# Ternary weights turned by transposing DMA instead of by TensorE, in a fused graph-and-expert layer

## What is computed

```python
def _bit_quant(W):
    scale = jnp.clip(jnp.mean(jnp.abs(W), axis=-1, keepdims=True), 1e-05, None)
    w_q = jnp.clip(jnp.round(W / scale), -1.0, 1.0) * scale
...
shared_out = jax.nn.silu(jnp.einsum('btd,fd->btf', h, sw1)) @ sw2.T
...
h1 = jax.nn.silu(jnp.einsum('btd,efd->ebtf', h, ew1))
eo = jnp.einsum('ebtf,edf->ebtd', h1, ew2)
```

## Time and profile before

| | |
|---|---|
| median of 3 runs | 772.42 us |
| the profiled execution | 770.02 us, span 768.4 us |
| TensorE busy | 691.9 us, 90% of the span |
| VectorE busy | 502.9 us, 65% |
| ScalarE busy | 409.0 us, 53% |
| GpSimd busy | 199.9 us, 26% |
| moved by DMA | 145.69 MB, mean 190 GB/s |

### The profile page before, as it was taken

One profiled execution on the slowest core, in us unless ns is written; L12 is line 12 of the kernel. 1 busy time (PEld: TensorE's weight loads), 2 busy tenths in 40 slices (PEclk: granted clock), 3 DMA queues, 4 the chain that ended last, 5 costly groups with the idle time before them and its releaser, 6 DMA issues.

```text
span 768.4 us, 17793 instructions
## 1 busy us (share of the span) xinstructions
PE 691.9 (90%) x5737; PEld 412.7 (54%) x5738; DVE 502.9 (65%) x1111; ACT 409.0 (53%) x716; POOL 199.9 (26%) x195
## 2 busy tenths in 40 slices
PE   0889988999999999999887669899989999999996
PEld 0334433554544554544333357677766777777773
DVE  4888876546655546788888776765674545454554
ACT  2334346759977775867466635335344444444441
POOL 1222210000000000177656433520020543434332
PEclk9999999999999999999989979999999999999999
DMA  8999951433546878767555554255338544444431
GB/s 354 420 376 378 351 199 40 151 140 110 192 171 234 279 261 283 231 218 224 201 197 192 192 179 154 82 184 163 120 112 110 154 138 129 132 132 124 133 108 36
DMA packets 55585, 145.69 MB, mean 190 GB/s; under 512 B 8814, under 2 KB 8814, under 8 KB 51440
## 3 DMA queue, kind: packets, MB, share of 16 engines
q1 hardware_dynamic: 41792, 115.64, 44.3%
q0 software_dynamic: 6960, 20.99, 8.5%
q10 hardware_dynamic: 6784, 8.42, 3.5%
HBM read 127.69 MB, written 19.16 MB: 191 GB/s over the span
## 4 chain that ended last, share of the span: by engine, by line
PE 58%; issue 14%; DVE 11%; DMA 6%; ACT 5%; POOL 4%; ACTq 1%; DVEq 1%; SPq 0%; POOLq 0%
PE bank L1417 17%; PE bank L1441 15%; PE bank L1280 7%; PE bank L1282 7%; PE bank L1281 7%; DMA work<-in_w 4%; PE bank L1314 2%; POOL dv L519 2%; PE bank L1404 2%; ACT junk L670 2%; DVE work L991 2%; DVE region L1086 1%; DVE work L1058 1%; DVE s L979 1%; ACT region L678 1%
## 5 line engine op out<-in xcount | busy, mean ns | idle before, releaser
L1441 PE MATMUL bank<-region,work 128*128 (+1 forms) x624 | 142.9, 383 | 5.1 <-DVE work L1140 3.6
L1417 PE MATMUL bank<-work,region 128*128 128x128 f16 x1984 | 118.4, 221 | 4.1 <-ACT work L794 2.9
L1417 PEld LDWEIGHTS bank<-work,region 128*128 (+1 forms) x1984 | 114.7, 99 | 10.5 <-issue 3.4
L1280 PE MATMUL bank<-zreg,work 128*128 (+1 forms) x256 | 98.8, 386 | 13.5 <-DVE work L1058 11.2
L1280 PE MATMUL bank<-region,work 128*128 128x512 f16 (+1 forms) x192 | 74.8, 390 | 29.4 <-DVE region L914 29.3
L1140 DVE SCALAR_TENSOR_TENSOR work<-work 128x512 f16<-128x512 f32 x78 | 57.0, 732 | 67.1 <-ACT work L807 67.1
L1441 PEld LDWEIGHTS bank<-region,work 128*128 128x128 f16 x624 | 58.9, 98 | 74.4 <-issue 6.4
L1281 PE MATMUL bank<-zreg,work 128*128 (+1 forms) x256 | 98.6, 385 | 0.0
L1282 PE MATMUL bank<-zreg,work 128*128 (+1 forms) x256 | 98.5, 385 | 0.0
L794 ACT ACTIVATE work<-bank 128x1024 f16<-128x1024 f16 x31 | 31.7, 1024 | 124.3 <-PE bank L1404 119.0
L534 POOL TENSOR_TENSOR rb<-rb,power 128x2 f32<-128x2 f32 x16 | 16.3, 1021 | 271.4 <-DVE rb L1052 271.3
(11 more groups left out here) (157 smaller groups left out, 1034.2 us busy)
## 6 DMA issues: line engine op xcount, KB each, us to landing
work<-in_w SPq DMA_DIRECT2D x62, 512.0 KB, 3.5
region<-in_adj SPq DMA_DIRECT2D x16, 1024.0 KB, 8.9
region<-in_adj_t SPq DMA_DIRECT2D x16, 1024.0 KB, 7.5
work<-in_adj_t SPq DMA_DIRECT2D x32, 384.0 KB, 4.1
zreg<-s_scratch SPq DMA_DIRECT2D x39, 256.0 KB
xb<-in_w SPq DMA_DIRECT2D x10, 512.0 KB, 3.2
zreg<-in_x SPq DMA_DIRECT2D x4, 1024.0 KB, 9.0
h_scratch<-hb POOLq DMA_DIRECT2D x16, 256.0 KB, 4.0
```

Source lines behind the costliest of these rows:

```text
L1280: nc.tensor.matmul(dst, a_hi, b_hi, start=start, stop=False, skip_group_check=True)
L1417: last = nc.tensor.matmul(ps_h[b][f // 4][:, (f % 4) * P:(f % 4 + 1) * P], w, ht[r][:, c:c + P], start=(f % 4 == 0 and d == 0 and h == 0), ...
L1441: last = nc.tensor.matmul(ps_y[b][:, :].rearrange("p (d c) -> p d c", d=DB), h1hl[:, b, h, f * P:(f + 1) * P], w, start=(f == 0 and h == 0 ...
```

## The change

`turn_w` and its calls are removed from TensorE, with `tr_ok`. SP issues instead one transposing DMA for each chunk, from `steps16` in SBUF to the chunk's final place in `w1t` or `w2t`, still as int16 steps; two semaphores `turned[0]`, `turned[1]` count them. ScalarE takes the sign in place there. [...] SP issues the turn of chunk q-3 right before the early load of chunk q, and that of chunk q-2 right before the load of chunk q in stage 3. Before the shared rows of h are loaded SP waits for the last turns.

```diff
+            def turn(chunk, b):
+                q, kind, c = chunk
+                dst = (w1t if kind == 1 else w2t)[:, ds(c * CHUNK, CHUNK)]
+                sp.wait_ge(tern_ok, q + 1)
+                sp.dma_start(dst.bitcast(I16).rearrange("p (k r) -> p k r", r=P), steps16[:, b, :], transpose=True
+                             ).then_inc(turned[b], 16)
...
             def load_early(rnd, s):
                 q, kind, c = early(rnd, s)
                 if q >= 3:
-                    sp.wait_ge(tern_ok, q - 2)
+                    turn(early_at(q - 3), (q - 3) % 2)
...
+                    if isinstance(m, int) and m == 0 and s < 2:
+                        for q in range(EARLY_CHUNKS - 3 + 2 * s, EARLY_CHUNKS - 1 + s):
+                            turn(early_at(q), q % 2)
+                    elif idle and s < 2:
+                        turn_later(g, m, s)
+                    elif not (idle or isinstance(m, int) and m == IDLE + 1 and s < 2):
+                        turn_later(g, m - (g == 2), s)
+                    if not idle:
                         load_w(later(g, m - (g == 2), s), s % 2)
...
             for b in range(2):
+                turn(later(2, MACROS - 2, 2 + b), b)
+            for b in range(2):
                 sp.wait_ge(tern_ok, 2 * CHUNKS - 1 + b)
...
-                sp.wait_ge(tr_ok, 2 * CHUNKS - 1 + b)
+                sp.wait_ge(turned[b], 16 * CHUNKS)
                 load_shared(b, b)
...
             def store_w(chunk, b):
 
                 q, kind, c = chunk
-                act.wait_ge(tr_ok, q + 1)
-                dst = w1t if kind == 1 else w2t
-                nc.scalar.activation(dst[:, ds(c * CHUNK, CHUNK)], pst16[b], ACT.Sign).then_inc(wt_ok, 1)
+                act.wait_ge(turned[b], 8 * (q - b) + 16)
+                dst = (w1t if kind == 1 else w2t)[:, ds(c * CHUNK, CHUNK)]
+                nc.scalar.activation(dst, dst.bitcast(I16), ACT.Sign).then_inc(wt_ok, 1)
...
                 if not first:
-                    dve.wait_ge(tr_ok, q - 1)
+                    dve.wait_ge(turned[b], 8 * (q - b))
                 for a in range(k):
 
                     cols = slice(a * width, (a + 1) * width)
-                    ins = nc.vector.tensor_scalar(steps16[:, b, cols], src[:, cols], thr[:, b, 0, a:a + 1], None,
-                                                  ALU.mult)
+                    words, rows = steps16[:, b, cols], src[:, cols]
+                    if kind == 1:
+                        words = steps16[:, b, :].rearrange("p (d a c) -> p a d c", d=DB, a=2)[:, a, :, :]
+                        rows = rows.rearrange("p (d c) -> p d c", d=DB)
+                    ins = nc.vector.tensor_scalar(words, rows, thr[:, b, 0, a:a + 1], None, ALU.mult)
...
-            def turn_w(chunk, b, first):
-
-                q, kind, c = chunk
-                pe.wait_ge(tern_ok, q + 1)
-                if not first:
-                    pe.wait_ge(wt_ok, q - 1)
-                for k in range(8):
-
-                    dst = (k % 4) * 2 + k // 4 if kind == 1 else k
-                    last = nc.tensor.transpose(pst[b][:, dst * P:(dst + 1) * P], tern[:, b, k * P:(k + 1) * P], ident[:, :])
-                last.then_inc(tr_ok, 1)
```

More of the change, by code:

```diff
@@ L252, in build @@
         tern_ok = sem("tern_ok")
-        tr_ok = sem("tr_ok")
+        turned = [sem("turned0"), sem("turned1")]
         wt_ok = sem("wt_ok")
@@ L381, in _, with early_at @@
             sp.dma_start(rt[:, :, :], router_t.rearrange("(b p) e -> p b e", p=P)).then_inc(small_in, 16)
+            def turn(chunk, b):
[4 more added lines that the diff above has]
+                             ).then_inc(turned[b], 16)
+            def early_at(q):
+                rnd = 0
+                while q >= early_count(rnd):
+                    q -= early_count(rnd)
+                    rnd += 1
+                return early(rnd, q)
             def load_early(rnd, s):
@@ L406, in _, with turn_later @@
                     load_early(rnd, s)
+            def turn_later(g, m, s):
+                if s >= 2:
+                    turn(later(g, m, s - 2), s % 2)
+                elif not (isinstance(m, int) and m == 0):
+                    turn(later(g, m - 1, s + 2), s % 2)
             def macro(g, m, first):
                 c0, nc_ = Y_GROUPS[g][0] * P, Y_GROUPS[g][1] * P
+                idle = isinstance(m, int) and m == IDLE
                 for s in range(STEPS):
@@ L417, in macro @@
                                  ).then_inc(at_loaded[s % 2], 16)
-                    if not (isinstance(m, int) and m == IDLE):
+                    if isinstance(m, int) and m == 0 and s < 2:
[6 more added lines that the diff above has]
+                    if not idle:
                         load_w(later(g, m - (g == 2), s), s % 2)
@@ L428, in _ @@
                 macro(g, m0, g == 0)
-                with sp.Fori(m0 + 1, m0 + NT // STEPS) as m:
+                if g:
+                    macro(g, m0 + 1, False)
+                with sp.Fori(m0 + 1 + (g > 0), m0 + NT // STEPS) as m:
                     macro(g, m, False)
+            for b in range(2):
+                turn(later(2, MACROS - 2, 2 + b), b)
             for b in range(2):
@@ L1336, in early_round @@
                     last.then_inc(rest_step, 1)
[L1337 to L1340, removed]
-                            chunk = early(0, EARLY - 1)
-                        else:
-                            chunk = (2 * EARLY + (EARLY + EARLY_W1) * (rnd - 2) - 1, 2, None)
-                        turn_w(chunk, (k8 - 1) % 2, first and k8 <= 2)
             add_identity(1, u_hi, True, left=(1, 2, 3, 4))
@@ L1360, in macro @@
                     b = s % 2
-                    late_turn = first and g == 1 and s == 1
-                    idle = isinstance(m, int) and m == IDLE
-                    if s and not (late_turn or idle):
-                        turn_w(later(g, m - (g == 2), s - 1), (s - 1) % 2, False)
-                    elif s == 0 and isinstance(m, int) and m == 0:
-                        turn_w(early(ROUNDS - 1, early_count(ROUNDS - 1) - 1), 1, False)
-                    elif s == 0 and not (isinstance(m, int) and m == IDLE + 1):
-                        turn_w(later(g, m - 1 - (g == 2 and not idle), STEPS - 1), 1, False)
                     pe.wait_ge(atlo_ok, STEPS * m + s + 1)
@@ L1380, in macro @@
                     last.then_inc(p2_step, 1)
-                    if late_turn:
-                        turn_w(later(g, m, 0), 0, False)
             for g in range(3):
@@ L1390, in _ @@
                     macro(g, m, False)
-            turn_w(later(2, MACROS - 2, STEPS - 1), 1, False)
             def rows_to_columns(n, r, shared):
```

## The result

The changed kernel takes 789.63 us (median of 4 runs, 789.16 to 790.27) against 772.45 us (4 runs, 771.42 to 774.01) for the kernel before: a ratio of 1.0217, 95% interval 1.0195 to 1.0238, slower by 17.2 us. The forecast was 784. Its profiled execution took 789.5 us.

A forecast was written before the change was run, and what follows sets the result against it. TensorE was taken to bound the early rounds and groups 0 and 1, the weight stream group 2. The terms -9 + 2 + 6 + 10 + 2.5 = +11.5 us took 770.0 to 781.5; 2.4 more to the median gave 784 us, range 757 to 880.

The forecast's parts named there:

- the cheap rival: SP's issue and the queue behind it: turns cost little and the kernel gets faster, 755 to 763 us; chance 0.31.
- the dear turn: Rival on the turning transfers: pieces, not bytes, cost; 813 us at 3 us a turn, 922 at 6.4; chance 0.26.
- The issue of a turn: On SP: issuing one 256 KB turn takes 1.3 us, reckoned from a price per piece for 1024 pieces.
- Its data: In SP's queue: the turn's data delay the load behind it by 1.0 us, between ends of 0.6 and 5.5.
- Early rounds: Rounds 0 to 3: TensorE loses the turns, -5.3 us in rounds 0 and 1, -3.8 in 2 and 3, together -9.
- Group 0: Stage 3, first group: the raw-buffer loop at 4.45 us a step replaces TensorE's 4.34 as the bound, +2 us.
- Group 1: Stage 3, second group: the raw-buffer loop takes 4.65 us a step against about 4.25 before, +6 us.
- the step of the loop: Raw-buffer loop of stage 3, two buffers, turn included: 4.45 us a chunk in group 0, 4.65 in group 1.
- Group 2: Stage 3, third group: the loop takes 4.75 us against 3.95 in the 12 steps with a chunk, +10 us.
- The end: End of stage 3: the last turn's issue and the loads of x stand ahead of the h loads, +2.5 us.
- TensorE's clock: Groups 0 and 1: more waits may lower the clock; a tenth of 3.9 us stays under 4.45, so no change.
- At nothing: VectorE's strided w1 write, ScalarE's sign from SBUF and the added waits on turns: no cost counted, sign 1 us in all.

The follow-up runs named there:

- two half turns: The changed kernel with each turn issued as two transposing transfers of 128 KB: ratio 1.0548 to the kernel before, changed part 370.8 us.

## Why the prediction was right and wrong

The direction and its cause were right: the turn stands in the loop over raw buffers, TensorE's gain is smaller than what the loop loses, and of the rivals neither the cheap nor the dear turn came. By its steps:

- *The issue of a turn*, 1.3 us: 1.24 measured, in the kernel's own row. The reason given (a price per piece) was wrong, as two half turns show.
- *Its data*, 1.0 us of delay for the load behind it: median landings grew by 0.3 to 0.8 us in stage 3, but by 1.9 us early. With a plain copy in the turn's place the early landing grew by 0.3 us only, to 3.6. The early load's issue grew from 0.33 to 0.58 us, which the prediction didn't have; it is 0.59 behind the plain copy, so it doesn't come from the turning.
- *Early rounds*, -9: -10.4 in the products, +6.0 in the lag, **-4.4** together. This step failed. I took 2.80 us a chunk, level with ScalarE, and counted the rounds' length by TensorE's steps; the stage ends when ScalarE has done its last chunk. With the landing measured the loop is (2.95 + 1.24 + 5.2 + 0.2) / 3 = 3.2 us, not 2.8.
- *Group 0*, +2: **+5.3**. *Group 1*, +6: **+11.2**. The term that was mis-sized is the step of the loop, 4.45 and 4.65 us; measured are 75.1 / 16 = 4.7 and 84.0 / 16 = 5.25. My loop held the raw buffers alone. The adjacency load stands behind turn and raw load on SP too, and a late `high` delays `low`, the products, and the next adjacency load. The text named the queue behind a waiting instruction and did not price it for `at`.
- *Group 2*, +10: **+6.8**. It was taken as 4.75 us a chunk. Why it is less was not tried.
- *The end*, +2.5: +3.1.
- *TensorE's clock*, at nothing: "a tenth of 3.9 us stays under the loop's 4.45". The mean of a stretch, 0.96 and 0.94 in groups 0 and 1, hid what happens in one step. After a wait of 3.26 us TensorE was granted the lower of its two levels, 1.2 GHz, for most of the next step:

```profile
314.54 0.61 PE L1316 MATMUL bank<-zreg,work 128*128 128x512 f16 x1 [3.26 <-DVE work L1094]
```

```profile
314.60:320.60 6.00, 6.00 (x15) 2.13 (x16) 2.57 (x9) 4.09 (x10) 0.00 (x0) 0.51 1.02 263
```

```profile
321.60 0.84 ACT L748 ACTIVATE work<-work 128x768 f16<-128x768 f32 x1 [1.48 <-PE bank L1318]
```

The matmuls of this step stand 0.43 us apart instead of 0.216, the step takes 6.8 us instead of 3.9, above the loop's 4.65, and ScalarE's `high` waits for it. Such steps added 3.2 us to TensorE's work in group 0 and 4.6 in group 1, and ScalarE waited 0.75 us for them in group 0 and 1.48 + 1.05 us in group 1. So some 0.75 and 2.5 us of the +5.3 and +11.2 can have come by this way; no run keeps the clock up to show how much did. Before the change no step of these groups ran at the lower level.
- *At nothing*: VectorE's write of w1 in the order of its final place costs nothing (652 ns a write for all forms together, 668 before). ScalarE's sign in place takes 1.04 us against 1.00. ScalarE waited for turns 4.3 us in 4 waits, VectorE 0.4.
- *"DMA engines are busy 0.46 to 0.75, so there is room"*, the argument for the cheap rival: they were busy 0.81 to 0.98 afterwards. 72 plain copies fitted with no measurable loss or gain; the turns take 2.5 times as much of the engines as the copies (1.61 against 0.64 us).
- The sum was +11.5 for a changed part that grew by 22.0. That the forecast of 784 lies only 5.6 us under the measured time is partly luck: it allowed 2.4 us from the profiled execution to the median, which the changed kernel doesn't show (789.5 against 789.6), and 2.6 us came back where nothing was changed.

Two rules of the Trainium skill were weighed. The Trainium skill, "Advanced Engine Details and Errata", X-Bar Transpose (TRN2), makes transposing transfers as fast as plain ones. What is like it here: the quickest turn landed 3.0 - 1.24 = 1.8 us after its issue, the quickest plain copy 2.3 - 0.49 = 1.8. What is not: a turn takes 1.61 us of all engines where a plain copy of the same bytes takes 0.64, which is 163 against 410 GB/s, and the rate that the Trainium skill gives there is 350 to 400; its issue is 2.5 times as long. The Trainium skill, "VectorE: DVE Perf Modes", advises TensorE for a 128 x 128 transpose where a PSUM destination will do (the section Rules for kernel authors; the prediction names The three transpose paths, which has the times). The result agrees with the advice. It does not agree with the 10.5 us that the prediction estimated from the time for one block: eight blocks in one instruction landed in 4.0 us.

## What to carry to other kernels

Work that is moved from the bounding engine to a DMA queue is paid in that queue's issue time, and at the place in the order where it is issued: ask for each load behind it which buffer loop it closes, and count every loop, not just the one of the moved data. A stage's gain is there only when the engine that makes the next stage's operand has finished too; look at who was waiting for whom at the boundary before. A low busy share of the DMA engines says little of what small transfers will do, and a high one afterwards doesn't say that bytes are the limit: take bytes away and see. And read the clock step by step: a mean of 0.94 over a stretch held a step at half speed that took 6.8 us instead of 3.9.

## What the runs showed of the hardware

- The issue of a transposing transfer held SP for 1.24 us for 256 KB and 1.21 us for 128 KB; a plain one for 0.49 us in one piece a partition, and 0.63 us for 128 KB in 512 pieces of 256 bytes.
- An early raw load right behind another transfer of the queue was issued in 0.58 us behind a turn and 0.59 us behind a plain copy, against 0.33 us with no transfer there; it landed after 5.2, 3.6 and 3.3 us.
- Of all 16 DMA engines' time 256 KB from SBUF to SBUF took 0.64 us in whole rows, 1.17 us in 256-byte pieces and 1.61 us turned, each to some 0.15 us, with the same count of packets for the last two. So by this measure about half of the extra time goes with the small pieces, the rest with the turning.
- Taking away 11 to 14% of the bytes in a stretch with a busy share of 1.01 left the share of the DMA engines at 0.99 and 0.95.
- After a wait of 3.26 us TensorE's granted clock was 0.51 for 6.0 us, and 14 of its matmuls of 512 columns stood 0.43 us apart instead of 0.216.
